# A tile's three pieces of scores made in a row, and their maximum taken by one VectorE instruction over three PSUM banks

## What is computed

```python
q = (x @ wq).reshape(b, n, heads, dh).transpose(0, 2, 1, 3)
k = (ctx @ wk).reshape(b, j, heads, dh).transpose(0, 2, 1, 3)
v = (ctx @ wv).reshape(b, j, heads, dh).transpose(0, 2, 1, 3)
sim = jnp.einsum('bhid,bhjd->bhij', q, k) * scale
a = jax.nn.softmax(sim, axis=-1)
out = jnp.einsum('bhij,bhjd->bhid', a, v)
```

## Time and profile before

| | us |
|---|---|
| median of 3 executions | 6163.31 |
| the profiled execution | 6137.53 |
| its span | 6135.7 |
| TensorE matmuls busy in it | 5702.6 (93%) |
| VectorE busy in it | 2809.0 (46%) |
| ScalarE busy in it | 3107.8 (51%) |
| GpSimd busy in it | 3112.7 (51%) |

### The profile page before, as it was taken

How to read it: one execution, slowest core, us unless ns; L and a number is a source line. 1 busy time by engine, 2 the same in 40 slices (tenths; PEclk the granted TensorE clock), 3 DMA queues, 4 the chain that set the end, 5 groups by cost and what they waited for, 6 DMA issues and landing times.

```text
span 6135.7 us, 92602 instructions
## 1 busy us (share of the span) xinstructions
PE 5702.6 (93%) x34384; PEld 4684.0 (76%) x34384; DVE 2809.0 (46%) x5170; ACT 3107.8 (51%) x7280; POOL 3112.7 (51%) x3472
## 2 busy tenths in 40 slices
PE   7999999999999999988999999799999999999998
PEld 5777777778778877776666666588888878888887
DVE  1444444444444444434555555354444554444452
ACT  1445554545455545553445454256555555555554
POOL 0444444444444444463556555166555655555565
PEclk8899999999999999997899999599999999999998
DMA  2000000000000000000001011000000000000000
GB/s 55 12 16 16 16 13 15 16 16 15 16 15 12 13 16 11 16 20 19 27 24 32 25 29 41 8 19 16 18 16 15 20 18 19 16 15 18 15 19 10
DMA packets 84429, 114.48 MB, mean 19 GB/s; under 512 B 42814, under 2 KB 64682, under 8 KB 83978
## 3 DMA queue, kind: packets, MB, share of 16 engines
q1 hardware_dynamic: 83978, 108.56, 6.1%
HBM read 104.06 MB, written 4.46 MB: 18 GB/s over the span
## 4 chain that ended last, share of the span: by engine, by line
PE 68%; DVE 14%; ACT 8%; DMA 6%; issue 3%; POOL 2%; POOLq 0%; ACTq 0%; SPq 0%; DVEq 0%
PE ps_c L689 13%; PE ps_s L1128 6%; PE ps_c L1070 6%; PE ps_u L1143 5%; PE ps_s L1130 5%; PE ps_s L1129 5%; DVE mpiece L1452 5%; PE ps_u L1144 5%; PE ps_u L1145 5%; PE ps_c L1089 3%; ACT p L1819 2%; DMA w_area<-recs 2%; ACT p_hi L1821 2%; DMA sums<-uT 1%; DMA srec<-sums 1%
## 5 line engine op out<-in xcount | busy, mean ns | idle before, releaser
L1608 POOL TENSOR_TENSOR p_lo<-p,p_hi 125x448 fp32r<-125x448 f32 (+2 forms) x2688 | 2718.8, 1020 | 2292.3 <-ACT p_hi L1821 1626.0
L1819 ACT ACTIVATE p<-ps_s 125x448 f32<-125x448 f32 (+2 forms) x2688 | 1326.1, 493 | 2086.0 <-PE ps_s L1130 1903.5
L1821 ACT ACTIVATE p_hi<-ps_s 125x448 fp32r<-125x448 f32 (+2 forms) x2688 | 1316.0, 490 | 0.0
L1452 DVE TENSOR_REDUCE mpiece<-ps_c 125x1 f32<-125x500 f32 (+1 forms) x1984 | 1234.7, 668 | 105.2 <-PE ps_c L1070 98.2
L1128 PE MATMUL ps_s<-q_hi,ctxT_hi 105*125 105x448 f32 (+3 forms) x2688 | 1010.5, 376 | 38.1 <-ACT p_hi L1821 17.8
L1070 PE MATMUL ps_c<-ctxT_hi,q_hi 96*125 96x500 f32 (+1 forms) x2112 | 856.4, 432 | 132.6 <-DVE mpiece L1452 114.8
L1143 PE MATMUL ps_u<-p_hi,ctx_hi 125*97 125x448 f32 (+2 forms) x2688 | 975.9, 363 | 3.7 <-ACT uT L1809 2.7
L1129 PE MATMUL ps_s<-q_lo,ctxT_hi 96*125 96x448 f32 (+2 forms) x2688 | 934.8, 348 | 0.0
L1130 PE MATMUL ps_s<-q_hi,ctxT_lo 96*125 96x448 f32 (+2 forms) x2688 | 932.1, 347 | 0.0
L1144 PE MATMUL ps_u<-p_hi,ctx_lo 125*96 125x448 f32 (+2 forms) x2688 | 924.9, 344 | 0.0
L1145 PE MATMUL ps_u<-p_lo,ctx_hi 125*97 125x448 f32 (+2 forms) x2688 | 923.4, 344 | 0.0
(11 more groups left out here) (231 smaller groups left out, 6002.7 us busy)
## 6 DMA issues: line engine op xcount, KB each, us to landing
ctx_raw<-in_ctx SPq DMA_DIRECT2D x96, 562.5 KB
pT<-recs SPq DMA_DIRECT2D x32, 420.0 KB, 3.3
w_area<-recs SPq DMA_DIRECT2D x32, 420.0 KB, 3.2
w_area<-recs SPq DMA_DIRECT2D x32, 168.0 KB, 3.3
cs<-in_ctx SPq DMA_DIRECT2D x192, 6.0 KB, 3.0
x_between<-x_out SPq DMA_DIRECT2D x32, 80.0 KB
x_in<-x_between SPq DMA_DIRECT2D x32, 80.0 KB
w_area<-in_L_xattn_wq SPq DMA_DIRECT2D x2, 800.0 KB, 5.8
```

The lines of the kernel that those rows point to most:

```text
L1452: z = V.tensor_reduce(mpiece[0:wide, k, r:r + 1], C(0, wide, n % banks(t), 0, PIECE), AX.X, ALU.max)
L1608: P.tensor_tensor(p_lo[0:kp, k % 3, 0:w], p32[0:kp, k % 2, 0:w], p_hi[0:kp, k % RING, 0:w].bitcast(F32), ALU.subtract).then_inc(*sig("pl_r ...
L1819: A(p32[0:kp, k % 2, 0:w], ps_s[0:kp, k % 2, 0:w], ACT.Exp, scale=DH[t.ph] ** -0.5)
L1821: A(p_hi[0:kp, k % RING, 0:w], ps_s[0:kp, k % 2, 0:w], ACT.Exp, scale=DH[t.ph] ** -0.5)\
```

## The change

In the first and the last phase the three pieces of a tile are now one step. TensorE waits once, for the tile before (`mp_ready` now counts tiles), and issues three matmuls in a row; only the third raises `mp_psum`. VectorE waits for that and reduces all three banks with one instruction over a view of 125 partitions x 3 x 500 (`CW`), into one column of `mpiece`. There are 9 steps numbered 1, 4, 7, ... on TensorE and 2, 5, 8, ... on VectorE where there were 27. The first tile now waits for all three pieces of `ctxT_lo` (`ctl_ready`), since it uses all three banks; before, the first matmul waited for one of them. The casts to `ctx_hi` come after the tile's reduction in whose numbers they fall, where they stood between single reductions. The middle phase keeps the old code.

```diff
-    "mp_psum": ((54, 24, 54), 0), "mp_ready": ((54, 24, 54), 0), "mx_ready": ((2, 2, 2), 0),
+    "mp_psum": ((18, 24, 18), 0), "mp_ready": ((18, 24, 18), 0), "mx_ready": ((2, 2, 2), 0),
...
+        def CW(n_rows):
+
+            return ps_c[0:n_rows, 0:512 * NPIECE].rearrange("p (r k) -> p r k", r=NPIECE)[:, :, 0:PIECE]
...
                 def maxima(t, b):
 
                     tiles, wide = MAX_TILES[t.ph]
-                    for k in range(tiles):
+                    for k in range(tiles if t.ph != 1 else 0):
+                        yield 1 + NPIECE * k
+                        if k == 0:
+                            pe.wait_ge(*got("ql_ready", t, per("ql_ready" if b else "qs_ready", t)))
+                            pe.wait_ge(*got("ctl_ready", t, NPIECE * (b + 1)))
+                        else:
+                            pe.wait_ge(*got("mp_ready", t, tiles * b + k))
+                        for r in range(NPIECE):
+                            z = mm(C(0, wide, r, 0, PIECE), q_hi[0:DC, b, wide * k:wide * k + wide],
+                                   ctxT_hi[0:DC, b, PIECE * r:PIECE * r + PIECE], start=True, stop=True)
+                        z.then_inc(*sig("mp_psum"))
...
+                    for k in range(tiles if t.ph != 1 else 0):
+                        yield 2 + NPIECE * k
+                        dve.wait_ge(*got("mp_psum", t, tiles * b + k + 1))
+                        V.tensor_reduce(mpiece[0:wide, k, 0:1], CW(wide), AX.XY, ALU.max).then_inc(*sig("mp_ready"))
+                        for n in range(NPIECE * k, NPIECE * k + NPIECE):
+                            if n in HI_AT[t.ph]:
+                                rounding(n)
...
-                    V.tensor_reduce(mneg[0:wide, 0:tiles], mpiece[0:wide, 0:tiles, :], AX.X, ALU.max, negate=True)\
+                    V.tensor_reduce(mneg[0:wide, 0:tiles], mpiece[0:wide, 0:tiles, 0:NPIECE if t.ph == 1 else 1], AX.X, ALU.max,
+                                    negate=True)\
```

More of the change, by code:

```diff
@@ L1058, in maxima @@
                     tiles, wide = MAX_TILES[t.ph]
-                    for k in range(tiles):
+                    for k in range(tiles if t.ph != 1 else 0):
[9 more added lines that the diff above has]
+                        z.then_inc(*sig("mp_psum"))
+                    for k in range(tiles if t.ph == 1 else 0):
                         for r in range(NPIECE):
@@ L1431, in maxima, with rounding @@
                     tiles, wide = MAX_TILES[t.ph]
-                    for k in range(tiles):
+                    def rounding(n):
+                        j = HI_AT[t.ph].index(n)
+                        if j == 0:
+                            dve.wait_ge(*got("cr_loaded", t, 16 * (b + 1)))
+                            if t.ph == 1 and b == 0 and t.it:
+                                dve.wait_ge(*got("pv_done", t, -(per("pv_done", t) // 2)))
+                        V.tensor_copy(ctx_hi[:, b, 4 * j:4 * j + 4, 0:DC],
+                                      ctx_raw[:, 4 * DC * j:4 * DC * (j + 1)].rearrange("p (c d) -> p c d", c=4))\
+                            .then_inc(*sig("ctx_hi"))
+                    for k in range(tiles if t.ph != 1 else 0):
[5 more added lines that the diff above has]
+                                rounding(n)
+                    for k in range(tiles if t.ph == 1 else 0):
                         for r in range(NPIECE):
@@ L1455, in maxima @@
                     yield 3 * tiles + 2
-                    dve.wait_ge(*got("mp_ready", t, NPIECE * tiles * (b + 1)))
-                    V.tensor_reduce(mneg[0:wide, 0:tiles], mpiece[0:wide, 0:tiles, :], AX.X, ALU.max, negate=True)\
+                    dve.wait_ge(*got("mp_ready", t, per("mp_ready", t) // 2 * (b + 1)))
+                    V.tensor_reduce(mneg[0:wide, 0:tiles], mpiece[0:wide, 0:tiles, 0:NPIECE if t.ph == 1 else 1], AX.X, ALU.max,
+                                    negate=True)\
                         .then_inc(*sig("mx_ready"))
```

## The result

The changed kernel takes **6512.4 us** (median of 4, 6490.87 to 6520.78) beside 6161.4 us for the kernel before in the same comparison: ratio **1.057, interval 1.0534 to 1.0607**, so 5.7% slower. The forecast was 6510 us. The profiled execution took 6520.8 us with a span of 6519.0, against a span of 6135.7 before.

The account below looks back on a forecast made before the run. The prediction took TensorE, 93% busy, as the bound. Its terms, 99 + 78 + 59 + 70 + 29 + 12 = 347 us, added to the profiled 6137.53 us and scaled by 1.0042 to the median, gave 6510 us, range 6370 to 6620.

Parts of the forecast that it names:

- The reduction: VectorE's one wide reduction of 1500 elements over three banks in the outer phases: 1.72 us.
- The round: A tile's maxima in the outer phases, from one release of the banks to the next: 2.75 us.
- the first batches: Maxima of first batches: 25.0 us each in the first phase, +99 together; 25.3 each in the last, +78 together.
- the four large terms: Added time in first and second batches of the first and last phases: +99, +78, +59 and +70 us.
- Second batches: Maxima of second batches: +59 us together in the first phase, +70 us in the last, 14 stretches each.
- The starts: Maxima alone at half clock at the two starts: 32.2 us each, +29 us for both.
- The middle phase and the gaps: Middle phase, which keeps its code, and other gaps between stretches: no added time, 0 us.
- TensorE's waits: A sign to look for: TensorE's waits for `mpiece` rise from 115 to some 300 us.
- That second batches cost nothing: Rival: VectorE and transfers already hold the second batches, so the change adds nothing there; 6374 us, chance 12%.
- That the wide reduction is no cheaper than three: Rival: the wide reduction takes 0.28 us more in some 460 waited rounds, +129 us; 6640 us, chance 6%.
- That it is faster: Rival: three banks read at twice the rate, deciding at a reduction of about 0.95 us; 6040 us, chance 2%.
- That the clock falls: Rival: new waits bring half clock to first batches' maxima, some 500 us more; 7010 us, chance 6%.

Follow-up runs that it names:

- The half read: The changed kernel with a reduction that reads only the first 250 of each bank's 500 scores, so maxima over half the keys; 6169.07 us, ratio 1.0082 to the kernel before.
- the run of second batches alone: The change in second batches of the first and last phases only, first batches as in the kernel before; 6262.44 us, ratio 1.0221 to the kernel before.
- the spread version: The changed kernel with its three matmuls back at their old places, one step apart, wide reduction kept; 7375.42 us, ratio 1.2061 to the kernel before.
- The steps: Kernels from before to the change: matmuls in a row 1.0215, banks given back together 1.0354, reductions after the third matmul 1.0715, merged into one instruction 1.057.

## Why the prediction was right

*The reduction.* 1.72 us was taken from the rows of 1120 and 448 elements, and 1719 ns is what the trace of after has. The slope there, 1.04 ns an element out of PSUM, held across a bank's edge. The half read (750 columns, 936 ns) lies on the same line. To pay the fixed share once instead of three times is worth 0.13 us a tile here: three queued reductions take 1.85 us. (What the prediction cites for it from the Trainium skill, "VectorE: DVE Perf Modes", section "The TRN2 errata", is said there of SBUF sources; for PSUM sources, as here, the section has the formula alone.)

*The round.* 2.75 us of parts, measured 2.75 and 2.76. This one number made the first batches come out: 25.0 forecast and 25.04 measured, 25.3 and 25.41 in the last phase, and the four large terms together 327 us where 306 were forecast, with the 16 us of later start that the forecast counts in its second batches.

*Second batches.* Forecast +59 in the first phase, counted from the old first matmul, so that the later start was in it. Measured +54 and +16 ahead, 70: 11 us too little, 0.8 us each. The clock was at its lower level for 98 us there against 65 before, where I had given 0.7 us a stretch, 10 in all, to slow rounds. In the change four of the 14 stretches stayed at the upper level and took 25.5 us; the other ten took 26.9 to 28.8, which is 24 us more in sum. How much of these 24 the kernel before had in its own second batches is not separated, so the 11 us are put down to the clock only by their size.

*The starts.* +27 for +29: 31.04 us instead of 32.2, at a granted clock of 0.50 as taken. The row of three takes 1.61 us there (timeline of the change, 174.45 to 176.06), where the prediction's 1.36 + 0.42 gave 1.78, and from row to row it is 3.43 us (174.45 to 177.88) and not 3.6.

*The middle phase and the gaps* were costed at nothing. They gave +22 us in the profiled pair, of which the middle phase's 8 is scatter and the gaps' 14 mostly so, as said above. With the 11 us of the second batches and 6 of the first this is the difference between the sum of 347 and the measured 387. The median was met all the same because the profiled execution of before was a quick one (6137.53 against 6163.31): the sum was short by 36 us on the profiled executions, and scaling to the median added 25. The profiled execution of the change was also a slow one, 8 us above its median. A part of the closeness of 6510 to 6512 is luck.

*TensorE's waits* for `mpiece` were to rise "to some 300 us": 336 in the rows, and 23 more in the middle phase, 359 beside the 115 of before.

*The rivals.* That second batches cost nothing: out, by the run of second batches alone. That the wide reduction is no cheaper than three: three queued ones took 1.85 us and 1.5 points more. That it is faster: at 0.94 us a reduction the kernel was still 0.8% behind, so even the deciding point of that rival was too kind. That it had left out what the row itself costs would explain this, but no run shows it. That the clock falls: for 20 us in all in the change's 30 first batches, where this rival had it fall throughout, but in the spread version for 512. The reason that the prediction gave against it does not hold as it stands: it saw the clock fall behind waits of 1.6 us and more, and in the change it fell five times behind waits of at most 0.9 us.

*What was wrong behind the right number.* The prediction speaks of one added cost, the lost overlap in the banks. The steps split it in three: the matmuls in a row (2.2 points), the banks held, with the edits that came along (1.4), and the late start of VectorE (3.6). Before I ran it I had expected the first to cost little. The sum was right because the round was followed as a whole.

## What to carry to other kernels

Where two engines hand a few banks to and fro, count the round from release to release before merging instructions: saving 0.13 us of fixed time a tile is worth nothing if the merged instruction must wait for all of its inputs and gives none back until its end. No run here gave the maxima more banks than their three (`ps_s` has two and `ps_u` three), so what a second set would have saved is not shown. Cover for a longer round has to come from somewhere, and a planner that moves it uncovers the work next door, so read the waits of the whole engine and not of the one line. And a single wait for a transfer in front of a busy handover costs twice where the clock falls after it; to move the waiting instruction by a few steps was the cheapest gain of this study.

## What the runs showed of the hardware that I had not expected

- Queued reductions overlap: single ones take 669 ns, but three in a queue took 1.85 us, so the second and third add 0.59 each. The fixed share that merging can save is therefore 0.07 us an instruction on VectorE, not the 0.16 that two single durations suggest.
- A reduction over three banks at once lies on the same line as one inside a bank: 624 ns for 448 elements in one bank, 936 for 750 and 1719 for 1500 in three. All fit 0.16 us and 1.04 ns an element, so the banks' edges bring no gain and no loss.
- TensorE's clock stayed at its upper level through a first batch with seven waits of at most 1.2 us, and was at the lower after waits of 1.61 us and 1.81 us. The waits inside the stretch alone do not decide it: in five of the 15 first batches of the first phase of the change it fell 8.1 to 8.4 us into the stretch, about where the third wait ends, and the other ten have the same three waits there (0.88, some 0.6 and 0.87 us) and kept the upper level. What decides was not measured.
